# Bit search for a rank threshold: packed counts in PSUM, sign sums on ScalarE, and settling steps between masks

## What is computed

```
S = relu(att[:, 0]);  S[..., 0] = 0;  S = S * (1 - eye(T))
FF = cumsum(S shifted down by one row, axis=1)
att = att - FF
FF_mod = where(causal, FF, inf)
rank = argsort(argsort(FF_mod, axis=-1))
keep = rank < minimum(memory_budget - 1, i + 1)      # memory_budget = int(2048 * 0.2) = 409
keep = keep | eye(T)
att = where(keep, att, -inf);  y = softmax(att) @ v
```

## Time and profile before

| | |
|---|---|
| times of three runs | 2983.0, 2986.77, 2960.94 us |
| profiled execution, span from its first to its last instruction | 2972.6 us |
| profiled execution, its own time | not given apart from the span |
| first mask of the search | 144.54 us |
| first operation of k = 15 (L859) | 251.55 us |
| threshold put together (L873) | 395.44 us |
| TensorE busy over the span | 2648.6 us, 89% |
| VectorE busy | 1845.0 us, 62% |
| ScalarE busy | 1787.0 us, 60% |
| mean granted TensorE clock | 0.948 |

### The profile page before, as it was taken

How to read it: one execution, slowest core, us unless ns; L and a number is a source line. 1 busy time by engine, 2 the same in 40 slices (tenths; PEclk the granted TensorE clock), 3 DMA queues, 4 the chain that set the end, 5 groups by cost and what they waited for, 6 DMA issues and landing times. The chain is left out here.

```text
span 2972.6 us, 75835 instructions
## 1 busy us (share of the span) xinstructions
PE 2648.6 (89%) x31084; PEld 1645.1 (55%) x31084; DVE 1845.0 (62%) x5185; ACT 1787.0 (60%) x3488; POOL 337.1 (11%) x710
## 2 busy tenths in 40 slices
PE   8998978888888799999998889999999999897596
PEld 3386955666666563222212456676676667655355
DVE  5599978778787574100001657777777787753862
ACT  2375856555566527999998227666666666532331
POOL 1100033222222010000000100000000000016016
PEclk8998979999999899999999899999999999898598
DMA  3140001001110202110000010000000000203103
GB/s 95 42 67 1 2 2 17 17 17 17 17 17 10 54 1 66 54 45 1 1 1 1 17 40 2 7 7 7 2 7 7 7 2 2 79 29 47 33 13 59
DMA packets 84736, 67.84 MB, mean 23 GB/s; under 512 B 40584, under 2 KB 73496, under 8 KB 84008
## 3 DMA queue, kind: packets, MB, share of 16 engines
q1 hardware_dynamic: 75944, 56.70, 8.0%
q0 software_dynamic: 8448, 6.30, 1.6%
HBM read 47.21 MB, written 19.96 MB: 23 GB/s over the span
## 5 line engine op out<-in xcount | busy, mean ns | idle before, releaser
L1733 ACT ACTIVATE arena<-ps 128x1024 f32<-128x1024 f32 x512 | 474.1, 1300 | 25.9 <-PE ps L1683 24.1
L1184 DVE CUSTOM_DVE_ANT_0 arena<-ps,arena 128x1024 f32<-128x1024 f32 (+7 forms) x384 | 349.7, 930 | 107.8 <-PE ps L1060 91.9
L2111 DVE CUSTOM_DVE_ANT_0 arena<-ps,arena 128x512 f32<-128x512 f32 (+3 forms) x640 | 371.2, 643 | 26.7 <-PE ps L1975 25.9
L1136 ACT ACTIVATE arena<-ps 128x1024 f32<-128x1024 f32 (+3 forms) x320 | 275.4, 895 | 133.4 <-PE ps L1093 129.9
L2068 ACT ACTIVATE arena<-arena 128x1152 f32<-128x1152 f32 (+15 forms) x256 | 306.4, 1199 | 63.4 <-DVE arena L2111 63.4
L1975 PE MATMUL ps<-arena 64*128 64x512 f32 (+3 forms) x1280 | 270.4, 547 | 3.5 <-ACT arena L2044 1.1
L1694 PE MATMUL ps<-arena 128*32 128x512 f32 x2048 | 273.0, 604 | 0.0
L2006 PE MATMUL ps<-arena 128*64 128x128 f32 x4352 | 262.3, 275 | 0.0
L2006 PEld LDWEIGHTS ps<-arena 128*64 128x64 f32 x4352 | 235.3, 137 | 33.4 <-issue 28.7
L887 PE MATMUL ps<-arena 128*128 128x256 bf16 (+1 forms) x2176 | 238.4, 273 | 14.7 <-DVE arena L859 9.3
L1088 PE MATMUL ps<-arena 64*128 64x64 f32 x4352 | 218.0, 232 | 19.4 <-ACT arena L1136 11.5
(11 more groups left out here) (298 smaller groups left out, 4095.0 us busy)
## 6 DMA issues: line engine op xcount, KB each, us to landing
arena<-scr_q SPq DMA_DIRECT2D x256, 32.0 KB
scr_s<-scr_f SPq DMA_DIRECT2D x1, 4096.0 KB, 17.7
arena<-scr_k SPq DMA_DIRECT2D x32, 128.0 KB
arena<-by_head_k SPq DMA_DIRECT2D x16, 192.0 KB
arena<-scr_s SPq DMA_DIRECT2D x16, 192.0 KB, 2.6
arena<-by_head_q SPq DMA_DIRECT2D x28, 96.0 KB
by_head_k<-arena SPq DMA_DIRECT2D x5, 512.0 KB, 4.5
scr_x<-arena SPq DMA_DIRECT2D x2, 1024.0 KB, 5.4
```

The costliest lines, as they stand in the source:

```text
L1136: e.activation(turned_block(u, kc), src, ACT.Exp, scale=-1.0).then_inc(exped, 1)
L1184: e.tensor_tensor_reduce(scored_block(u, g)[:, lo:hi], PS[:, 1024 * (k % 2):1024 * (k % 2) + hi - lo], NF[t][:, lo:hi], -1.0, mxs[:, col - ...
L1733: e.activation(PTR[k % RS], PS[:, at(n):at(n) + 1024], ACT.Sigmoid, scale=float(1 / np.sqrt(8.0))).then_inc(weighed, 1)
L2111: e.tensor_tensor_reduce(slot(u, t, g)[:, lo:hi], PS[:, base(step) + 512 * g:base(step) + 512 * g + hi - lo], bias, -1.0, mxs[:, col - 1:c ...
```

## The change

- The five narrowest tiles, 7, 4, 3 (set 0) and 6, 5 (set 1), get no mask and no fold any more. ScalarE counts them alone (L984 of the changed kernel): `Sign(edge - halves[t])` over all columns of the tile, read as uint16 from SBUF, with `edge`, the candidate less 0.5, as bias from a column, and the sum into `cnt`. The bf16 signs go to one of two scratch places. The limits of these tiles are written for a sum of signs.
- The other eight tiles form four pairs: 8 with 15 and 11 with 12 (set 0), 9 with 14 and 10 with 13 (set 1). The two masks of a pair are folded into one bank, the second with `IDP`, 2048 times the identity, so that one sum holds both counts (L973, Identity with the bias column `spread`, 2^23/256 per column, which puts the sum beside 2^23, so that the low bits of the float are the two counts).
- VectorE has four settling steps per set: `unpack` (bitwise, takes the count of the pair's first tile out of the sum, L866), `compare` (L871), `raise_value` (L877), `next_edge` (L884). They stand between the masks of the other set: `unpack` behind its second mask, `compare` behind the third, `raise_value` and `next_edge` behind the fourth.
- At k = 15 `widen` takes the place of the last three (five small operations), and the rebuilds of the narrow tiles come behind their sign sums.
- Ten more small fills and one more cast stand ahead of the search. ScalarE's order in a step is `reads`: sign 7, sign 4, pair 0, sign 3, pair 1 for set 0, and sign 6, pair 0, sign 5, pair 1 for set 1.

```diff
-            sets = [[15, 12, 11, 8, 7, 4, 3], [14, 13, 10, 9, 6, 5]]
+            ones_of, packs_of, direct_of = [[8, 11], [9, 10]], [[15, 12], [14, 13]], [[7, 4, 3], [6, 5]]
...
+            reads = {0: [("sign", 7), ("sign", 4), ("pair", 0), ("sign", 3), ("pair", 1)], 1: [("sign", 6), ("pair", 0), ("sign", 5), ("pair", 1)]}
...
-                def settle(k, i):
-                    lo, hi = edges(i)
-                    w.wait_ge(counted, count_no[k, i, sets[i][-1]] + 1)
...
-                    e.tensor_tensor(hit[:, lo:hi], cnt[:, lo:hi], lim[:, lo:hi], ALU.is_le).then_inc(settled, 1)
-                    w.wait_ge(settled, settle_no(k, i) - 1)
-                    e.scalar_tensor_tensor(value[:, lo:hi], hit[:, lo:hi], float(1 << bit), value[:, lo:hi], ALU.mult, ALU.add).then_inc(settled, 1)
+                def unpack(k, i):
+                    ones, packs, _, _ = columns_of(i)
+                    for x in reads[i]:
+                        w.wait_ge(counted, count_no[(k, i) + x] + 1)
+                    e.tensor_scalar(cnt.bitcast(I32)[:, ones], cnt.bitcast(I32)[:, packs], 0x7FF, 0x4B000000, ALU.bitwise_and, ALU.bitwise_or).then_inc(settled, 1)
+
+                def compare(k, i):
+                    every = columns_of(i)[3]
+                    w.wait_ge(settled, settled_no(k, i, 1))
+                    e.tensor_tensor(hit[:, every], cnt[:, every], lim[:, every], ALU.is_le).then_inc(settled, 1)
+
+                def raise_value(k, i):
+                    every = columns_of(i)[3]
+                    value, bit = (high, 14 - k) if k < 15 else (low, 31 - k)
+                    w.wait_ge(settled, settled_no(k, i, 2))
+                    e.scalar_tensor_tensor(value[:, every], hit[:, every], float(1 << bit), value[:, every], ALU.mult, ALU.add).then_inc(settled, 1)
+
+                def next_edge(k, i):
...
+                    w.wait_ge(settled, settled_no(k, i, 3))
+                    e.tensor_scalar(edge[:, direct], value[:, direct], step, None, ALU.add).then_inc(settled, 1)
...
+                for k in range(NC + 1):
                     for i in range(2):
-                        if k:
-                            w.wait_ge(settled, settle_no(k - 1, i))
-                        for t in sets[i]:
...
-                        if i:
-                            settle(k, 0)
-                        elif k:
-                            settle(k - 1, 1)
+                        steps = []
+                        if k or i:
+                            j = (k - 1, 1) if i == 0 else (k, 0)
+                            steps = [unpack, widen] if j[0] == 15 else [unpack, compare, raise_value, next_edge]
...
+                        tiles_ = masked_of[i] if k < NC else []
+                        for n, t in enumerate(tiles_):
+                            mask(k, i, t)
+                            if n and steps:
+                                steps.pop(0)(*j)
+                        for f in steps:
+                            f(*j)
...
             def search_tensor(e, w):
...
+                    for t, into in ((one, IDB), (pack, IDP)):
+                        n, W = mask_no[k, i, t], 128 * (t + 1)
+                        w.wait_ge(masks, n + 1)
+                        for c0 in range(0, W, 256):
+                            c1 = min(c0 + 256, W)
+                            m = e.matmul(bank(g % 8, c1 - c0), into, tally[n % 7][:, c0:c1], start=(t == one and c0 == 0), stop=(t == pack and c1 == W))
+                        m.then_inc(folded, 1)
...
             def search_scalar(e, w):
...
-                    e.activation(junk[n % 8], bank(n % 8, 256), ACT.Copy, accum_out=cnt[:, s:s + 1]).then_inc(counted, 1)
+                        e.activation(junk[len(read) % 4], bank(g % 8, 256), ACT.Identity, bias=spread, accum_out=cnt[:, s:s + 1]).then_inc(counted, 1)
...
+                        if k:
+                            w.wait_ge(settled, settled_no(k - 1, i, 4))
...
+                        if signed[x % 2]:
+                            w.wait_ge(counted, signed[x % 2][-1] + 1)
+                        e.activation(signs[x], halves[x], ACT.Sign, bias=edge[:, s:s + 1], scale=-1.0, accum_out=cnt[:, s:s + 1]).then_inc(counted, 1)
```

More of the change, by code:

```diff
@@ L815, in stage1, with columns_of, settled_no @@
             NC = 32
-            counts = [(k, i, t) for k in range(NC) for i in range(2) for t in sets[i]]
-            count_no = {x: n for n, x in enumerate(counts)}
-            def edges(i):
-                return place[sets[i][0]], place[sets[i][-1]] + 1
-            def settle_no(k, i):
-                return 2 * (2 * k + i + 1)
+            UNIT, PACK, ALL = 8388608.0, 2048.0, KEEP - 1
+            spread = SM[:, 624:625]
+            above, edge = SM[:, 628:632], SM[:, 528:544]
+            groups = [(k, i, x) for k in range(NC) for i in range(2) for x in range(2)]
+            masks_order = [(k, i, t) for k in range(NC) for i in range(2) for t in masked_of[i]]
+            mask_no = {x: n for n, x in enumerate(masks_order)}
+            reads = {0: [("sign", 7), ("sign", 4), ("pair", 0), ("sign", 3), ("pair", 1)], 1: [("sign", 6), ("pair", 0), ("sign", 5), ("pair", 1)]}
+            counts = [(k, i) + x for k in range(NC) for i in range(2) for x in reads[i]]
+            count_no = {x: n for n, x in enumerate(counts)}
+            group_no = {x: n for n, x in enumerate(groups)}
+            SETTLES = {k: 4 if k != 15 else 6 for k in range(NC)}
+            def columns_of(i):
+                lo, mid = place[ones_of[i][0]], place[packs_of[i][0]]
+                last, hi = place[direct_of[i][0]], place[direct_of[i][-1]] + 1
+                return slice(lo, mid), slice(mid, last), slice(last, hi), slice(lo, hi)
+            def settled_no(k, i, step):
+                return sum(2 * SETTLES[x] for x in range(k)) + i * SETTLES[k] + step
             def search_vector(e, w):
@@ L876, in search_tensor @@
+            N_BUILT = 4 + 2 * 2 + 5 + 2
+            lowered_no = {t: N_BUILT + n + 1 for n, t in enumerate(masked_of[0] + direct_of[0] + masked_of[1] + direct_of[1])}
             def search_tensor(e, w):
-                w.wait_ge(built, 4)
+                w.wait_ge(built, N_BUILT)
                 w.wait_ge(f_relu, upto[15])
                 w.wait_ge(f_copied, upto[15])
-                for n, (k, i, t) in enumerate(counts):
-                    W = 128 * (t + 1)
-                    w.wait_ge(masks, n + 1)
-                    if n >= 8:
-                        w.wait_ge(counted, n - 7)
-                    for c0 in range(0, W, 256):
-                        c1 = min(c0 + 256, W)
-                        m = e.matmul(bank(n % 8, c1 - c0), IDB, tally[n % 7][:, c0:c1], start=(c0 == 0), stop=(c1 == W))
-                    m.then_inc(folded, 1)
+                for g, (k, i, x) in enumerate(groups):
+                    one, pack = pairs_of[i][x]
+                    if g >= 8:
+                        w.wait_ge(counted, count_no[groups[g - 8][0:2] + ("pair", groups[g - 8][2])] + 1)
+                    for t, into in ((one, IDB), (pack, IDP)):
[5 more added lines that the diff above has]
+                        m.then_inc(folded, 1)
@@ L890, in search_scalar @@
             def search_scalar(e, w):
                 w.wait_ge(part, 10)
-                for n, (k, i, t) in enumerate(counts):
-                    s = place[t]
-                    w.wait_ge(folded, n + 1)
-                    if n >= 8:
-                        w.wait_ge(counted, n - 7)
-                    e.activation(junk[n % 8], bank(n % 8, 256), ACT.Copy, accum_out=cnt[:, s:s + 1]).then_inc(counted, 1)
+                w.wait_ge(built, N_BUILT)
+                w.wait_ge(f_high, 13)
+                read, signed = [], {0: [], 1: []}
```

96 lines of the change are left out of this document (70 added, 26 removed).

## The result

The changed kernel takes 2957.94 us (median of 13 runs, 2952.98 to 2969.56); the kernel before took 2976.39 beside it (13 runs, 2960.94 to 2999.44). The ratio is 0.9951, with a 95% interval of 0.993 to 0.9972: half a per cent faster. The forecast was 2963 us.

The account below looks back on a forecast made before the run. TensorE and VectorE bound the old bit together (7.105 us); ScalarE would bind next at 6.52. 31 bits x 0.58 plus 1.65 saves 19.8 us: span 2952.8, plus 10.4 around it, 2963 us; own range 2957 to 2969, overall 2944 to 2986.

Parts of the forecast that it names:

- Which engines are relieved and which binds next: Ordinary search bits: TensorE falls to 5.47 us and VectorE to 5.3; ScalarE binds at 6.52.
- ScalarE's durations: ScalarE per bit: five sign sums like attention's exponentials, 4.63 us, plus four packed sums of 0.472, 1.89; together 6.52.
- So ScalarE wins by 0.07 only; here a small error turns the bound: Set 1's half of a bit: ScalarE's own work, 2.90 us, just exceeds the hand-over chain, 2.83.
- The chain of set 1's half: From set 0's last sum through `unpack`, masks 10 and 13 and seven matmuls to set 1's last sum: 2.83 us.
- Rival A: Ordinary bits: ScalarE is cheaper through overlap or a hidden column bias; 6.0 us per bit, 2947 us; chance 0.13.
- Rival B: Ordinary bits: late steps and TensorE restarts lengthen the chain; set 1's half 3.13, bit 6.75, total 2970 us; chance 0.15.
- Rival C: Ordinary bits: VectorE's small steps and ScalarE's waits swallow the gain; 2983 us; chance 0.04.
- Rival D: TensorE in ordinary bits: pauses lower its clock; with half the bits cold, 47 us slower, 3028 us; chance 0.06.
- Bit 15: Bit 15, where VectorE is full: five narrow masks leave, rebuilds stay; 1.65 us less.
- The clock's return in the next bit is the same in both: Bit 16: TensorE's clock recovery after bit 15 costs both kernels the same, so no difference was counted.
- Start and end at zero within 1 us: Search ends: extra fills (0.3 to 0.5 us) and final steps (0.4) stand against TensorE's shorter backlog; zero within 1 us.
- The sum: Whole search: 31 ordinary bits x 0.58 = 18.1 us plus 1.65 from bit 15, 19.8 us less.

Follow-up runs that it names:

- unpack late: Changed kernel with `unpack` behind the third mask of the other set instead of the second: 6.40 us per bit, ratio 0.9853.
- one wait: Changed kernel with `unpack` waiting once, for the last count of its set, instead of each in turn: 6.515 us per bit, ratio 0.9954.
- no bias: Changed kernel with packed sums taken by Copy without bias column, upper half of the threshold zero: 6.34 us per bit, 2978.45 us in one run.
- warm: Changed kernel with 20 small matmuls ahead of each mask's fold in bit 15 only: 6.61 us per bit, ratio 0.9944.
- unpacked: Changed kernel with each of the eight masks in its own bank with its own Copy sum: 7.48 us per bit, 3000.53 us in one run.
- balanced, warm: Changed kernel with tiles 3 and 4 masked and packed, `unpack` behind the third mask, one wait, 20 matmuls per mask in bit 15: 5.956 us per bit, ratio 0.9911.

## Why the prediction was right, and where its terms were off

The median came out 5 us under the forecast and inside its own narrow range (2957 to 2969). Hitting that range was partly luck. The forecast stands on the 2983.0 of three runs; 13 runs put the kernel before at 2976.39, and from there the same saving ends at 2956.6. The saving itself was put at 19.8 us and came as 15.8 in the search, 14.6 by the ratio and 18.5 between the medians. Point by point:

- **Which engines are relieved and which binds next**: right. TensorE 40.00 to 35.40, VectorE 38.03 to 31.99, ScalarE 32.18 to 39.05 of 40 us. TensorE's 52 matmuls and VectorE's cost were hidden, as said.
- **ScalarE's durations**: right for each kind. Sign sums of 1137 to 713 ns where the exponentials of the earlier trace rows gave 1144 to 708; packed sums 463 where 472 was worked out. Signs from uint16 cost what exponentials from float32 do. The sum of all was put at 6.52 and is 6.40 ("unpack late"): the packed sums take 0.45 to 0.46 of distance instead of 0.47, and each sign sum some 0.01 less than its row.
- **"So ScalarE wins by 0.07 only; here a small error turns the bound"**: it turned. This is the step that failed. The chain of set 1's half was put at 2.83 us and took 3.05, ScalarE's own work there 2.85 instead of 2.90. The 0.22 consist of: `unpack` 0.68 behind the sum's start instead of 0.60, which "one wait" shows to be the price of waits one by one (0.09 to 0.10); 0.08 for the compare, which stands between masks 10 and 13 and which the prediction had left out, though it had the order before it; and about 0.07 from the mask's end to the sum, 1.04 instead of 0.97. By the trace's records most of that is the fold itself: tile 13's seven matmuls run from 306.60 to 307.52, 0.93 instead of 0.88, since the seven of the earlier trace rows were tile 12's, the last of them only 128 columns wide. Set 0's half, 3.57 for a predicted 3.62, was held by ScalarE as said.
- **The two errors cancelled.** The bit was predicted at 6.52 as pure ScalarE time. It is 6.61: 6.40 of ScalarE's own, and 0.2 of its waiting for the chain. The forecast of the size was right to 0.09 us per bit in part by luck, because a term that was too large stood in for one that was missing.
- **Rival A** (cheaper ScalarE, 6.0 per bit): refuted. A sign sum of 896 columns, 1.03 long, is followed by the next operation 1.03 us after its start; the bias column does not hide either ("no bias", 0.09 each). The Trainium skill, page "ScalarE: Activation LUTs", section "What ACT_TABLE_LOAD costs", says that back-to-back activations overlap by about 93 ns. The trace shows that overlap and shows where it goes: the read of the accumulator starts 0.10 before the sign sum's end (305.89 and 305.99), the next sum 0.09 before the read's end (305.99 and 306.08), and the read, 0.19 long, uses up what the two overlaps give. So a sum costs its full duration, as the earlier trace rows had it.
- **Rival B** (a longer chain, 6.75): its mechanism is what happened, at a smaller size. It named the step after the mask and TensorE's restart. The first was real in another form (the row of waits, the compare), 0.2 us in all against its 0.3. The restart was slow too, 0.15 us from the end of tile 10's mask (305.85) to its first matmul (306.00) where 0.05 was taken; it cost next to nothing, because tile 13's mask ended only at 306.52 and its first matmul started at 306.60.
- **Rival C** (no gain) fell with the period. **Rival D** (cold clock): refuted. TensorE stands still for 0.61 us in every bit (its weight loads for 0.81 and 0.35) and keeps a granted clock of 1.00 from 310 to 350. The Trainium skill's page "TensorE: Matmul & The Clock Gate" warns, in "A second HAM failure mode: psum-queue depth-cycling", of a clock that swings under short idle times between groups. Ordinary bits show the pattern and no swing. In the search only 3.4 us of the first bit and the stretch from within bit 15 into bit 16 are at 0.50, as before.
- **Bit 15**: 1.65 predicted, 1.49 measured; the five widening steps that had been left out are the likely rest, which was not tried. "The clock's return in the next bit is the same in both" was wrong by 0.76: before, bit 16 was 1.07 over an ordinary bit, now 1.83. Part of it is that more of the bit was slow: before, the granted clock was back at 282.8, after 5.6 us of bit 16, and now after 6.6. In "one wait" it was 5.0 us, and bit 16 exceeds an ordinary one by 1.32, so one microsecond more is worth some 0.3, as an estimate. That a bit of 6.6 us also hides less of the slow matmuls than one of 7.1 is the likely rest and was not shown.
- **Start and end at zero within 1 us**: the fills cost 0.34, the tail gave 1.0.
- **The sum**: 19.8 us predicted, 15.8 in the search; the difference of 4.0 is 29 x 0.095 = 2.8 from the period, 0.85 from bit 16, 0.54 from the first bit, which gained next to nothing, 0.16 from bit 15, 0.3 from the one long bit and 0.34 from the fills, less 1.0 at the tail.

The value that was not forecast: the change went past its best point. Prediction and trace both had ScalarE as the new bound with TensorE and VectorE each some 1 us free per bit (6.52 against 5.47 and 5.3), which was the hint that two narrow tiles belong back on them.

## What to carry to other kernels

When work is moved from two full engines to a third, work out each engine's need per period and stop where they meet: here two of five tiles given back, with the waiting step one mask later, doubled the gain (6.61 to 6.01 us per bit). Where two limits come within 0.1 us, follow the chain instruction by instruction in the issue order of each engine, with the small ones between, and count what a row of waits ahead of an instruction costs. Read a small gain from the period in the trace; the whole time of this kernel moves by more for reasons outside the change.

## What the runs showed of the hardware that had not been expected

- Waits for several values of one semaphore ahead of a single instruction cost time even when all but the last had been reached: 0.13 us from the release to the instruction with four or five, 0.04 with one, and 0.10 us per bit. The last value was waited for in a wait instruction of its own, 0.05 long.
- ScalarE's operations that take a sum stand at their full duration from each other: 1.03 after 1.03 us at 896 columns (304.96 to 305.99), 0.45 to 0.46 for the packed sums. In "unpack late" the same operations are recorded 0.07 us longer at the same distance.
- The time at which the search begins moves by 12.6 us (134.5 to 147.1) between profiles, with the granted clock from 30 to 120 us between 0.94 and 0.79, in kernels that are the same up to there. That the clock is the cause was not tested.
- In the profiles of the changed kernel (both), "no bias" and "warm", one ordinary bit, bit 24, is 0.3 us longer than the others: tile 10's mask starts 0.38 us behind `unpack` instead of 0.08 (332.04 and 331.66). The kernel before, "unpacked" and "one wait" have none. Its cause stays open.
- The granted clock fell within a pause of 3.77 us after a stretch at 0.98, and its mean was 0.66 over the bit that followed ("balanced, warm"); it fell within one of 3.48 too, and the mean was 0.76 ("warm"). A pause of 0.61 us in each ordinary bit left it at 1.00.
